# Routing of a mixture-of-experts stage by batch, with tiles given out in order, a GpSimd subtraction and weights read in place

## The chip, the cores and the metric

The kernel runs on one core of one Trainium2 chip. The metric is the device time of that core in microseconds, lower is better. Each number of a profile comes from one profiled execution of the program.

## What is computed

The input `x` has 4 batches of 512 rows of 128 float32 values, and there is a context of 32 rows per batch. Eight layers are added to `x` one after the other, each on the row-normalised `x`:

```python
x = x + L0_xattn(layernorm(x), ctx)      # layer 0: attention, 8 heads, windows
x = x + L0_ffn(layernorm(x))             # layer 1: 8 experts, hidden 512, 1 expert a row
x = x + L1_xattn(layernorm(x), ctx)      # layer 2: attention, 16 heads
x = x + L1_ffn(layernorm(x))             # layer 3: 16 experts, hidden 256, 3 experts a row
x = x + L2_xattn(layernorm(x), ctx)      # layer 4: attention, 16 heads, causal mask
x = x + L2_ffn(layernorm(x))             # layer 5: dense, ternary weights
x = x + L3_xattn(layernorm(x), ctx)      # layer 6: attention, 16 heads, mask
x = x + L3_ffn(layernorm(x))             # layer 7: a table looked up by cluster and tile

# layer 1: top = argmax(logits + gate_b + expert_bias); out = relu(x@w1[e] + b1[e]) @ w2[e] + b2[e] for e = top
# layer 3: g = softmax(x @ gate); keep the 3 largest of 16, divide by their sum;
#          out = sum over the 3 of g[e] * (relu(x@W1[e] + b1[e]) @ W2[e] + b2[e])
```

## The kernel before

**Tiles.** A tile is 128 rows, so there are 16 tiles of `x`, four in each batch. Everything is float32. The program is written by hand for each engine, and the order of the lines is the order of each engine's work. Semaphores are waited on between engines.

**The two expert layers** (1 and 3) work on rows sorted by expert. TensorE computes logits for a batch (`logits`, L1421 to L1430). VectorE then does `gating` (L793 to L853) once for all 16 tiles. It finds the largest logit of each row by `first_largest` (L777 to L790), once for layer 1 and three times for layer 3, and writes one-hot choices. Layer 3 also takes a softmax, for which ScalarE does the exponential (L1285). TensorE's `ranks` (L1576 to L1584) counts by matmul with a triangle of ones how many rows chose each expert so far, in 17 matmuls. VectorE's `route` (L855 to L891) turns that into a slot number for each row and the expert number `es` of each tile of slots. Each expert owns whole tiles. Layer 1 has 24 tiles of slots, layer 3 has 64.

**Scatter and gather.** GpSimd issues indirect DMAs of one tile each. `scatter` (L450 to L457) writes the normalised rows to `xbuf` in DRAM: 16 DMAs for layer 1, 48 for layer 3. It waits on `s_slot`, which `route` raises once for the layer. `gather` (L459 to L465) reads the results back from `ybuf`, as many DMAs. The first gather of a layer waits until all groups of four tiles of the layer are stored. Its destination is the weight buffer `wall`, so the load of layer 3's weights (L410 on SP) waits until layer 1's gathered rows have been added. Between gathers GpSimd does `power` (L440 to L448), the square root of each layer norm: two small operations and one of some 1 us.

**The expert loop** (`moe`) has bodies of 8 tiles. SP loads groups of four tiles from `xbuf` and stores groups to `ybuf` (L386 to L392). TensorE does for tile s: `turn` (a transpose, L1597), then `hidden` for tile s-1 (L1605), then `second` for tile s-2 (L1614). A matmul of 128x128 float32 appears as two instructions in the trace. ScalarE copies the transposed tile (L1253) and does the ReLU (L1260). VectorE reads the eight expert numbers of a body into registers (L953) and for each tile copies the expert's w1 (L926), b1 (L927), w2 (L932) and b2 (L933) out of the whole set of weights with a register in the address, and adds the bias to a finished tile (L917). In layer 1 a tile has 4+4 matmuls and one transpose, in layer 3 it has 2+2 and one transpose.

**Attention** (`period`) is a pipeline over 16 tiles. TensorE makes scores (L1479), VectorE takes the row maximum (L735) and subtracts it (L739), ScalarE does the exponential (L1186), TensorE transposes (L1484), ScalarE copies (L1190), TensorE multiplies (L1495), VectorE normalises (L748, L752) and after four tiles adds to `x` (L556) and takes the statistics of the next norm (L521 to L528). In layer 6 VectorE also applies a mask by a minimum (L733). In layers 2 and 4 the gathered rows of a batch are added (`add_experts`, L893 to L908) in the middle of the attention's pipeline.

**Order around the experts.** Before the loop of layer 1, VectorE does `gating(1)`, `route(1)`, `prepare(2)` (attention weights), `prepare5` and `prepare7` (weights of the layers 5 and 7). Before the loop of layer 3 it does `gating(3)`, `route(3)`, `prepare(4)`, `prepare(6)` and a masked copy (L972). GpSimd's order is:

```python
for l in MOE:
    scatter(l)
    for r in range(2):
        pool.wait_ge(s_ys[r], 16 * (tile_before[l] + SLOT_TILES[l]) // BODY)
    gather(l, 0, 0)
    gather(l, 0, 1)
    for b in range(1, B):
        gather(l, b, 0)
        power(4 * l + 3 + b)
        gather(l, b, 1)
```

## Time and profile before

| | before |
|---|---|
| median of 3 runs | 740.15 us (739.88 to 740.39) |
| the profiled execution, its own time | 738.92 us |
| its span in the trace | 737.1 us |
| TensorE busy | 449.4 us (61%) |
| VectorE busy | 389.1 us (53%) |
| ScalarE busy | 242.0 us (33%) |
| GpSimd busy | 192.3 us (26%) |
| mean granted TensorE clock | 0.768 of full |

Some 1.8 us of the execution's own time lie around the span. "Busy" leaves out register, branch and semaphore instructions. A row of the timeline gives start, duration, engine, line, operation, output and inputs, and in brackets the idle time before it and what ended it. Two neighbouring instructions of VectorE can overlap in the rows by their tails, so what an instruction costs in a row of others is the distance from its start to the next start.

### The profile page before, as it was taken

The numbers are of one execution on the slowest core, as the hardware profiler recorded it, in microseconds if no ns is written. First come the engines' busy times: TensorE is split into PE (matmuls) and PEld (weight loads), VectorE is DVE, ScalarE is ACT, GpSimd is POOL, SyncE is SP. The second block draws the span as 40 slices with busy tenths as digits, with TensorE's granted clock in tenths as the row PEclk, the third lists the DMA queues.
The fourth block names the chain that finished last, engine by engine and source line by source line (L and its number), as shares of the span: only waits on it lengthen the run. The fifth ranks groups of instructions, "written<-read, shape, count | busy, mean of one in ns | idle before, by whom it ended". The sixth has DMA issues, their size and how long they took to land.

```text
span 737.1 us, 9512 instructions
## 1 busy us (share of the span) xinstructions
PE 449.4 (61%) x2662; PEld 353.8 (48%) x2662; DVE 389.1 (53%) x1346; ACT 242.0 (33%) x634; POOL 192.3 (26%) x250
## 2 busy tenths in 40 slices
PE   1935964699268862650068888025578998887070
PEld 1834562499236752410067777013455675774050
DVE  2343538465246836720036666044675659965856
ACT  0011101266144640020046666013334465553023
POOL 3010206200352110277700000586631120013002
PEclk9965557699779975675579999556787999997555
DMA  6493001221110700011123333111100000000001
GB/s 178 103 313 124 0 1 36 64 59 45 49 29 23 270 1 0 11 50 53 53 76 101 99 85 85 50 50 35 36 15 1 1 2 0 1 1 1 0 0 57
DMA packets 55884, 39.86 MB, mean 54 GB/s; under 512 B 8900, under 2 KB 50837, under 8 KB 55718
## 3 DMA queue, kind: packets, MB, share of 16 engines
q1 hardware_dynamic: 51750, 31.01, 14.2%
q0 software_dynamic: 4096, 8.40, 3.9%
q8 instruction: 17, 0.28, 0.2%
q14 instruction: 21, 0.17, 0.1%
HBM read 24.18 MB, written 15.20 MB: 53 GB/s over the span
## 4 chain that ended last, share of the span: by engine, by line
PE 35%; DVE 22%; POOL 15%; issue 10%; DVEq 8%; ACT 6%; DMA 3%; SPq 1%; POOLq 0%; ACTq 0%
POOL xbuf L457 8%; PE bank L1605 6%; PE bank L1614 5%; PE bank L1479 4%; POOL wall L465 3%; DVE e_sb L739 2%; ACT xn L1171 2%; POOL rstd L446 2%; DVE mx L735 2%; DVE stats L521 2%; PE bank L1382 2%; PE bank L1469 2%; PE bank L1582 2%; PE bank L1484 1%; PE bank L1510 1%
## 5 line engine op out<-in xcount | busy, mean ns | idle before, releaser
L465 POOL DMA_INDIRECT wall<-ybuf,slots x64 | 61.5, 961 | 172.1 <-DMA ybuf<-h_sb 96.0
L1260 ACT ACTIVATE r<-bank,b1s 128x128 f32<-128x128 f32 x224 | 67.3, 365 | 49.8 <-PE bank L1605 49.8
L457 POOL DMA_INDIRECT xbuf<-h_sb,slots x64 | 63.4, 991 | 70.8 <-DVE slots L890 51.9
L1605 PE MATMUL bank<-on,e_sb 128*128 128x128 f32 x448 | 70.4, 290 | 13.3 <-DVE b1s L927 12.8
L445 POOL TENSOR_SCALAR nmr<-mv 128x4 f32<-128x4 f32 x32 | 7.8, 244 | 237.8 <-DVE veps L528 236.0
L1605 PEld LDWEIGHTS bank<-on,e_sb 128*128 128x128 f32 x448 | 59.2, 198 | 21.6 <-DVE b1s L927 20.5
L917 DVE TENSOR_TENSOR h_sb<-bank,oT 128x128 f32<-128x128 f32 x88 | 25.5, 289 | 81.8 <-PE bank L1614 81.8
L1614 PE MATMUL bank<-eT,r 128*128 128x128 f32 x448 | 66.1, 280 | 0.6 <-issue 0.6
L1614 PEld LDWEIGHTS bank<-eT,r 128*128 128x128 f32 x448 | 57.8, 194 | 1.7 <-issue 1.1
L1469 PE MATMUL bank<-ident,xn 128*128 128x128 f32 x64 | 13.1, 340 | 74.5 <-ACT xn L1171 74.3
L1597 PE MATMUL bank<-ident,h_sb 128*128 128x128 f32 x88 | 24.7, 286 | 54.3 <-DMA h_sb<-xbuf 54.3
L1171 ACT ACTIVATE xn<-x,nmr,rstd 128x128 f32<-128x128 f32 x64 | 26.3, 481 | 68.6 <-POOL nmr L448 68.6
L1479 PE MATMUL bank<-VW,xnT_all 128*128 128x512 f32 x64 | 45.5, 818 | 5.1 <-ACT xnT_all L1179 3.2
L1495 PE MATMUL bank<-vB,eT 128*128 128x36 f32 x384 | 47.1, 271 | 0.0
L1190 ACT COPY eT<-bank 128x512 f32<-128x512 f32 x48 | 28.1, 584 | 57.7 <-PE bank L1484 57.7
L1495 PEld LDWEIGHTS bank<-vB,eT 128*128 128x128 f32 x384 | 46.9, 194 | 0.0
L1469 PEld LDWEIGHTS bank<-ident,xn 128*128 128x128 f32 x64 | 8.6, 169 | 78.0 <-ACT xn L1171 78.0
L1253 ACT COPY on<-bank 128x128 f32<-128x128 f32 x88 | 23.6, 269 | 65.0 <-PE bank L1597 64.7
L926 DVE COPY e_sb<-wall 128x256 f32 (+1 forms) x88 | 28.9, 328 | 21.9 <-ACT r L1260 11.6
L1597 PEld LDWEIGHTS bank<-ident,h_sb 128*128 128x128 f32 x88 | 12.9, 149 | 56.7 <-DMA h_sb<-xbuf 56.7
L735 DVE TENSOR_REDUCE mx<-bank 128x16 f32<-128x512 f32 x48 | 33.1, 689 | 13.1 <-PE bank L1479 11.0
L1484 PEld LDWEIGHTS bank<-ident,e_sb 128*128 128x128 f32 x192 | 25.7, 152 | 25.0 <-issue 15.0
(262 smaller groups left out, 928.3 us busy)
## 6 DMA issues: line engine op xcount, KB each, us to landing
wall<-in_w SPq DMA_DIRECT2D x4, 2048.0 KB, 12.3
h_sb<-xbuf SPq DMA_DIRECT2D x22, 256.0 KB, 2.8
ybuf<-h_sb SPq DMA_DIRECT2D x22, 256.0 KB, 2.3
xbuf<-zero SPq DMA_DIRECT2D x16, 256.0 KB, 3.7
x<-in_x SPq DMA_DIRECT2D x4, 256.0 KB, 3.7
xbuf<-h_sb,slots POOLq DMA_INDIRECT x64, 2.2
wall<-ybuf,slots POOLq DMA_INDIRECT x64, 2.5
b2all<-in_L_ffn_b SPq DMA_DIRECT2D x1, 1024.0 KB, 15.4
```

Source lines behind the costliest of these rows:

```text
L457: nc.gpsimd.indirect_dma_start(xbuf[0:SLOT_TILES[l] * P], bass.IndirectOffsetOnAxis(slots[:, c:c + 1], 0), tile_of(xn_all, t), None).then_ ...
L465: nc.gpsimd.indirect_dma_start(tile_of(yg, t * K + k), None, ybuf[0:SLOT_TILES[l] * P], bass.IndirectOffsetOnAxis(slots[:, c:c + 1], 0)).t ...
L735: v.tensor_reduce(m, s, AX_X, ALU.max)
L1171: i = a.activation(tile_of(dst, w), tile_of(x, b * W + w), ACT.Identity, bias=nmr[:, w:w + 1], scale=rstd[:, w:w + 1])
L1260: i = a.activation(hT[:, (u % 2) * 512 + c * P:(u % 2) * 512 + (c + 1) * P], bank[2 + u % 2][:, c * P:(c + 1) * P], ACT.Relu, bias=b1s[:, ...
L1469: i = nc.tensor.transpose(tile_of(xT_ps, w), tile_of(src, w), ident[:, :])
L1479: mm(s_ps[t % 2][:, :], tile_of(xnT_all, t), aB[l][:, (t // W) * 512:(t // W + 1) * 512], start=True, stop=True).then_inc(s_s, 1)
L1484: i = nc.tensor.transpose(tile_of(e_ps[t % 2], c), e_sb[:, (t % 2) * 512 + c * P:(t % 2) * 512 + (c + 1) * P], ident[:, :])
L1495: i = mm(o_ps[p % 2][:, at + c * VC:at + (c + 1) * VC], eT[:, (t % 2) * 512 + c * P:(t % 2) * 512 + (c + 1) * P], vB[l][:, ((t // W) * 4 + ...
L1597: nc.tensor.transpose(bank[4 + u % 2][:, 0:P], tile_of(xs, u), ident[:, :]).then_inc(s_xt, 1)
L1605: h = mm(tile_of(bank[2 + u % 2], c), w1s[:, (u % R) * n + c * P:(u % R) * n + (c + 1) * P], tile_of(xsT, u % 2), start=True, stop=True)
L1614: y = mm(bank[6 + u % 2][:, 0:P], hT[:, (u % 2) * 512 + c * P:(u % 2) * 512 + (c + 1) * P], w2s[:, (u % R) * n + c * P:(u % R) * n + (c + ...
```

## The change

- **Routing by batch.** `gating` and `route` take a batch (4 tiles) and run four times a layer, and so do `ranks` (5 matmuls) and, in layer 3, the exponential. `route` gives tiles of slots out in order: an expert that has room left in its last tile fills it first, and a batch adds new tiles behind those of the batches before. It therefore carries `room`, `last_end` and `ends` from batch to batch. In layer 3 the three largest come from the instructions `max` and `max_index`, one each for every tile, where `first_largest` was called three times.
- **Scatter by batch.** GpSimd scatters a batch as soon as its slots are known. In layer 3 the first batch's scatter stands before `power(14)` and `power(15)`, inside attention 2.
- **Gather by batch.** A batch can only have used the first `LIMIT` tiles: 11, 15, 19, 23 of 24 in layer 1, and 27, 39, 51, 63 of 64 in layer 3. Its gather waits for these alone, that is for 3, 4, 5, 6 groups of four tiles in layer 1 and for 7, 10, 13, 16 in layer 3. The gathers of batches 0 to 2 stand before the `power` of the next norm. Destinations are other buffers, and SP's wait for `s_gad` goes.
- **w2 in place.** VectorE no longer copies w2. TensorE loads the expert numbers of a body into its own registers (from `es_late`, shifted by two tiles) and reads w2 out of `wall` with a register in the address of each matmul of `second`.
- **GpSimd subtraction.** In layer 6 VectorE's minimum writes to SBUF (`s_sb`), the maximum reads from there, and GpSimd subtracts.
- **Moved.** `prepare5` and `prepare7` go from before layer 1's loop to before layer 3's loop, behind `prepare(4)` and `prepare(6)`. `prepare(2)` still stands before layer 1's loop.

The diff, cut to its core:

```diff
+LIMIT = {l: [min(SLOT_TILES[l], (512 * TOPK[l] * (b + 1) + MOE[l][0] * (P - 1)) // P) for b in range(B)] for l in MOE}
...
-        yg = wall
+        yg = {1: [vZ[:, b * S:(b + 1) * S] for b in range(B)],
+              3: [h_sb[:, B * S:B * S + 3 * S], vZ[:, 0:3 * S], vZ[:, B * S:B * S + 3 * S], wall[:, 0:3 * S]]}
...
-                    sp.wait_ge(s_gad, 4)
...
+            def scatter(l, b, part):
+                pool.wait_ge(s_slot, (b + 1) if l == 1 else B + b + 1)
+                if l == 1 and b == 0:
+                    pool.wait_ge(s_zero, loads["s_zero"])
+                for w in (2 * part, 2 * part + 1):
+                    for k in range(TOPK[l]):
+                        t = b * W + w
+                        nc.gpsimd.indirect_dma_start(xbuf[0:LIMIT[l][b] * P], bass.IndirectOffsetOnAxis(slots[:, k * T + t:k * T + t + 1], 0), tile_of(xn_all, t), None).then_inc(s_sc_x, 16)
...
             def gather(l, b, part):
                 K = TOPK[l]
+                groups_needed = -(-LIMIT[l][b] // GT)
+                if part == 0:
+                    for r in range(2):
+                        pool.wait_ge(s_ys[r], 16 * (tile_before[l] // BODY + (groups_needed + 1 - r) // 2))
...
+            for n in range(7):
                 power(n)
+            for part in range(2):
+                scatter(1, 0, part)
+            power(7)
+            for b in range(1, B):
+                for part in range(2):
+                    scatter(1, b, part)
+            for b in range(3):
+                gather(1, b, 0)
+                gather(1, b, 1)
+            power(8)
+            power(9)
+            gather(1, 3, 0)
+            gather(1, 3, 1)
+            for n in range(10, 14):
+                power(n)
+            scatter(3, 0, 0)
+            power(14)
+            scatter(3, 0, 1)
+            power(15)
+            for b in range(1, B):
+                for part in range(2):
+                    scatter(3, b, part)
+            for b in range(3):
+                gather(3, b, 0)
+                gather(3, b, 1)
+            power(16)
+            gather(3, 3, 0)
+            power(17)
+            add_bo(0)
+            gather(3, 3, 1)
...
+            def subtract(t):
+                g = att_before[6] * W + t
+                pool.wait_ge(s_mx, t + 1)
+                if t >= 2:
+                    pool.wait_ge(s_e, g - 1)
+                nc.gpsimd.tensor_tensor(tile_of(e_sb, t % 2, 512).rearrange("p (h j) -> p h j", h=H),
+                                        tile_of(s_sb, t % 2, 512).rearrange("p (h j) -> p h j", h=H),
+                                        mx[:, (t % 2) * H:(t % 2 + 1) * H].unsqueeze(2).to_broadcast([P, H, SK]), ALU.subtract).then_inc(s_sub, 1)
...
+            def gating(l, b):
...
+                v.tensor_reduce(most, logit, AX_X, ALU.max)
+                dve.drain()
+                v.tensor_tensor(tiles(gv), logit, most.unsqueeze(2).to_broadcast(w_), ALU.subtract).then_inc(s_gsub, 1)
+                dve.wait_ge(s_gexp, b + 1)
...
+                for w in range(W):
+                    v.max(top[:, w * 8:(w + 1) * 8], gv[:, w * E:(w + 1) * E])
+                dve.drain()
+                for w in range(W):
+                    v.max_index(top_i[:, w * 8:(w + 1) * 8], top[:, w * 8:(w + 1) * 8], gv[:, w * E:(w + 1) * E])
...
+            def route(l, b):
+                dve.wait_ge(s_rank, (b + 1) if l == 1 else B + b + 1)
+                v.tensor_copy(rk[:, 0:n + E], rank_bank(l, b)[:, 0:n + E]).then_inc(s_rk, 1)
...
+                v.tensor_copy(slots[:, :].rearrange("p (k t) -> p k t", k=3)[:, 0:K, b * W:(b + 1) * W],
+                              slot_f[:, 0:K * W].rearrange("p (k w) -> p k w", k=K)).then_inc(s_slot, 1)
+                reached = esc[:, 0:NS * E].rearrange("p (s e) -> p s e", e=E)
+                v.tensor_tensor(reached, number[:, 0:NS].unsqueeze(2).to_broadcast([1, NS, E]), ends[0:1, 0:E].unsqueeze(1).to_broadcast([1, NS, E]), ALU.is_ge)
+                dve.drain()
+                v.tensor_reduce(es_n[:, 0:NS], reached, AX_X, ALU.add)
...
+                if b == B - 1:
...
+                    v.tensor_copy(es_late[:, 2:NS + 2], es_f[:, 0:NS]).then_inc(s_es, 1)
+                    v.tensor_copy(es[:, 0:NS], es_f[:, 0:NS])
...
-            norm(5, 1, tile_of(xn_all, 1, S))
+            stats_of(5, 1)
+            gating(1, 0)
+            normed(5, 1, tile_of(xn_all, 1, S))
             add_y(0, 2)
-            norm(6, 2, tile_of(xn_all, 2, S))
+            stats_of(6, 2)
+            route(1, 0)
+            normed(6, 2, tile_of(xn_all, 2, S))
+            gating(1, 1)
             add_y(0, 3)
-            norm(7, 3, tile_of(xn_all, 3, S))
+            stats_of(7, 3)
+            route(1, 1)
+            normed(7, 3, tile_of(xn_all, 3, S))
+            gating(1, 2)
+            route(1, 2)
+            gating(1, 3)
+            route(1, 3)
...
                 if l == 6:
-                    v.tensor_tensor(s, s, cap6[:, t * SK:(t + 1) * SK].unsqueeze(1).to_broadcast([P, H, SK]), ALU.min)
+                    if t >= 2:
+                        dve.wait_ge(s_sub, g - 1)
+                    kept = tile_of(s_sb, t % 2, 512).rearrange("p (h j) -> p h j", h=H)
+                    v.tensor_tensor(kept, s, cap6[:, t * SK:(t + 1) * SK].unsqueeze(1).to_broadcast([P, H, SK]), ALU.min).then_inc(s_cs, 1)
                     dve.drain()
+                    v.tensor_reduce(m, kept, AX_X, ALU.max).then_inc(s_mx, 1)
+                    return
...
-                        v.tensor_copy(w2s[:, (u % R) * n:(u % R + 1) * n], wall[:, bass.ds(e * n + WHALF, n)])
...
             prepare(2)
+            moe(1)
+            add_experts(1, 1)
+            stats_of(norm_no(2, 1), 1)
+            for t in range(-1, 14):
+                period(2, t)
+            gating(3, 0)
+            period(2, 14)
+            route(3, 0)
+            for t in range(15, 18):
+                period(2, t)
+            gating(3, 1)
+            period(2, 20)
+            route(3, 1)
+            for b in (2, 3):
+                gating(3, b)
+                route(3, b)
+            prepare(4)
+            prepare(6)
+            v.copy_predicated(cap6[:, :], mask_u8[:, :], neg3[:, :])
             for stage in range(4):
                 prepare5(stage)
             prepare7()
...
+            def ranks(l, b):
+                pe.wait_ge(s_sel, (b + 1) if l == 1 else B + b + 1)
...
+                mm(out_[:, 0:(W + 1) * E], tri[:, :], gsel[:, 0:(W + 1) * E], start=True, stop=False, skip_group_check=True)
+                for t in range(W):
+                    i = mm(out_[:, (t + 1) * E:(W + 1) * E].rearrange("p (n e) -> p n e", e=E), ones[:, :],
+                           gsel[:, t * E:(t + 1) * E].unsqueeze(1).to_broadcast([P, W - t, E]), start=False, stop=(t == W - 1), skip_group_check=True)
...
-                pe.wait_ge(s_wd, s + (tb + 1))
...
-                               w2s[:, (u % R) * n + c * P:(u % R) * n + (c + 1) * P], start=(c == 0), stop=(c == C - 1))
+                               wall[:, bass.ds(e * n + (WHALF + c * P), P)], start=(c == 0), stop=(c == C - 1))
...
                 def body(i, peeled):
+                    experts = experts_of(i * BODY, BODY)
...
-                            second(s - 2, (u - 2) % BODY, peeled and u < 4)
+                            second(s - 2, (u - 2) % BODY, peeled and u < 4, experts[u])
```

On TensorE and ScalarE the exponentials, `ranks(3, b)` and `prepare5` are placed to match: `gate_exp(b)` after the periods 13, 17, 21 and 25 of attention 2, `ranks(3, b)` after the periods 14, 18, 21 and 24. On ScalarE the normalising of a batch for layer 3 (L1171, periods 13, 17, 21) stands ahead of `gate_exp`. On TensorE `prepare(2)` stands ahead of layer 1's loop as before.

## Rows read from the trace of the kernel before

**Rows 1.** Busy time by stretch: experts of layer 1, of layer 3, attention 6.

```profile
core 0: us, PE busy (x) PEld busy (x) DVE busy (x) ACT busy (x) POOL busy (x), PEclk, DMA share, GB/s
139.60:190.50 50.90, 48.40 (x408) 47.04 (x408) 28.83 (x119) 31.45 (x120) 0.00 (x0) 0.97 0.17 49
374.00:462.00 88.00, 75.73 (x574) 67.69 (x574) 56.71 (x310) 53.34 (x191) 0.00 (x0) 0.97 0.31 87
607.00:655.00 48.00, 41.80 (x257) 31.21 (x256) 42.87 (x92) 27.27 (x54) 4.46 (x10) 0.96 0.00 1
```

**Rows 2.** Timeline of VectorE: first additions behind each expert loop.

```profile
200.16 0.70 DVE L899 TENSOR_TENSOR x<-x,wall 128x512 f32<-128x512 f32 x1 [9.83 <-DMA wall<-ybuf,slots]
...
481.39 3.57 DVE L906 SCALAR_TENSOR_TENSOR x<-wall,gk,x 128x128 f32<-128x128 f32 x12 [19.49 <-DMA wall<-ybuf,slots]
```

**Rows 3.** Timeline of GpSimd: scatters in layers 1 and 3, an addition.

```profile
134.58 0.96 POOL L457 DMA_INDIRECT xbuf<-h_sb,slots  x1 [0.30 <-issue]
...
323.80 1.02 POOL L457 DMA_INDIRECT xbuf<-h_sb,slots  x1 [0.30 <-issue]
...
496.33 1.27 POOL L470 TENSOR_TENSOR x<-x,bo 128x512 f32<-128x512 f32 x1
```

**Rows 4.** Chain that ended last, layer 3: start us, us, what.

```profile
370.28 2.86 DMA h_sb<-xbuf
```

**Rows 5.** Timeline of TensorE, ScalarE, VectorE ahead of layer 1's loop.

```profile
86.46 1.71 PE L1429 MATMUL bank<-gw,xnT_all 128*128 128x8 f32 x8
...
105.41 5.32 PE L1582 MATMUL bank<-gsel,ones 128*128 128x128 f32 x32
...
123.11 0.58 ACT L1242 COPY VW<-bank 128x512 f32<-128x512 f32 x1 [0.78 <-PE bank L1559]
...
114.49 2.50 DVE L603 TENSOR_TENSOR vZ<-kT,mask 128x512 f32<-128x512 f32 x4 [0.16 <-issue]
```

**Rows 6.** Timeline of VectorE: steps of route in layers 1 and 3.

```profile
111.80 0.22 DVE L871 TENSOR_REDUCE first<-cmp_ 128x8 f32<-128x64 f32 x1
112.09 0.17 DVE L873 TENSOR_TENSOR ends<-first,ntile 128x8 f32<-128x8 f32 x1
112.18 0.17 DVE L874 TENSOR_SCALAR base<-first 128x8 f32<-128x8 f32 x1
...
302.23 1.20 DVE L879 TENSOR_TENSOR A<-number,ends 1x1024 f32<-1x1024 f32 x1
```

**Rows 7.** Timeline: ScalarE's norm in attention 2; VectorE's weight preparation.

```profile
257.11 1.63 ACT L1171 ACTIVATE h_sb<-x,nmr,rstd 128x128 f32<-128x128 f32 x4
...
307.46 0.29 DVE L595 TENSOR_REDUCE wqs<-wq 128x1 f32<-128x128 f32 x1 [0.16 <-issue]
...
322.58 0.28 DVE L926 COPY e_sb<-wall 128x256 f32 x1
...
117.60 0.69 DVE L616 SCALAR_TENSOR_TENSOR ab<-wfc 128x512 f32<-128x512 f32 x1
...
137.94 0.15 DVE L677 TENSOR_SCALAR temp<-temp 128x1 f32<-128x1 f32 x1
```

**Rows 8.** Timeline of TensorE and VectorE in layer 3's loop.

```profile
386.00 0.71 PE L1605 MATMUL bank<-on,e_sb 128*128 128x128 f32 x4 [0.92 <-DVE b1s L927]
...
387.00 0.27 PE L1597 MATMUL bank<-ident,h_sb 128*128 128x128 f32 x1
...
388.00 0.27 PE L1597 MATMUL bank<-ident,h_sb 128*128 128x128 f32 x1
...
396.88 0.71 PE L1605 MATMUL bank<-on,e_sb 128*128 128x128 f32 x4 [1.11 <-DVE b1s L927]
...
385.58 0.29 DVE L926 COPY e_sb<-wall 128x256 f32 x1 [1.09 <-ACT r L1260]
...
388.02 0.29 DVE L926 COPY e_sb<-wall 128x256 f32 x1 [0.20 <-issue]
```

**Rows 9.** Groups of instructions of VectorE in attention 6.

```profile
L739 DVE TENSOR_TENSOR e_sb<-bank,mx 128x512 f32<-128x512 f32 x16 | 11.1, 692 | 1.2
```

More of the change, by code:

```diff
@@ L499, in _ @@
+            for n in range(24, 27):
+                power(n)
+            for t in range(T):
+                subtract(t)
+                if t == 2:
+                    power(27)
+                if t in (9, 13):
+                    power(28 + (t - 9) // W)
+            power(30)
+            power(31)
             pool.wait_ge(s_c7, loads["s_c7"])
@@ L962, in _ @@
             prepare7()
-            moe(1)
-            add_experts(1, 1)
-            stats_of(norm_no(2, 1), 1)
-            for t in range(-1, 21):
-                period(2, t)
-            gating(3)
-            route(3)
-            prepare(4)
-            prepare(6)
-            v.copy_predicated(cap6[:, :], mask_u8[:, :], neg3[:, :])
             moe(3)
@@ L1649, in _ @@
                 prepare(6, stage)
+            for stage in range(3):
+                prepare5(stage)
             moe(3)
```

398 lines of the change are left out of this document (212 added, 186 removed).

## The prediction

> **What bounds the kernel now.** I read the page's slices first, then the chain of waits, then the timeline by engine around each gap. No engine is busy throughout. The time lies in stretches in which one thing is waited for.
>
> Around both expert layers GpSimd's indirect DMAs stand alone. Each takes 0.96 us and 0.30 us between two [rows 3], 1.26 us in all: 16 before layer 1's loop (20 us), 48 before layer 3's (61 us). Layer 3's rows are then loaded at 370.28 and landed at 373.1 [rows 4]. Behind the loops the first additions wait 9.8 us and 19.5 us for gathers [rows 2]. In layer 1's loop TensorE is busy 48.4 of 50.9 us. In layer 3's it is busy 75.7 of 88.0 us and in attention 6 it is 41.8 of 48.0 us, with VectorE at 42.9 [rows 1].
>
> **The change part by part**, against the profiled execution's own 738.92 us. The 1.8 us around the span stay. The median shown is 1.2 us higher.
>
> *A. Ahead of layer 1's loop: +6.4.* A drained step of VectorE on small operands costs 0.29 us, a second operation beside one 0.09 [rows 6]. A batch of layer 1 has a gating of 8 steps, which I take at 0.27 (2.1 us), and a route of some 13 to the slots (4.1) with a tail for the expert numbers (1.4). Ranks are 10 instructions, which at 5.32 us for 32 [rows 5] make 1.7, with the semaphores 2.0. The first logits end at 87.2: four matmuls (8 instructions, 1.71 us) from 85.6, where the output matmul before them ends, near 86.46, where they begin today [rows 5]. Batch 0's slots come at 102.0, since w_out(3), 4.1 us of TensorE, stands before its ranks. After that a batch takes 10 to 11 us: gating, ranks and route in series and the norm between. The slots stand at 113.3, 124.4 and 134.4, and VectorE is through at 136.4. The last four scatters would let the loop begin at 143.4. But `prepare(2)` follows on the same VectorE. It took from 114.49 to 123.7 [rows 5], 9.2 us beside the scatters, and now it has no cover: 145.6. Loading registers on TensorE takes another 0.9 (E), less 0.5 for ScalarE's last copy. The loop begins at 146.0 in place of 139.6. The scatters that get hidden are paid back by that chain.
>
> *B. Layer 1's loop: +1.* TensorE sets it, so VectorE's lost copy buys nothing. Register arithmetic is costed in E.
>
> *C. Behind layer 1: -11.2.* Three batches are gathered in the loop (3, 4 and 5 of 6 groups needed). The 9.8 us go. Another 1.4 go because the addition of batch 1, also late for its gather, made VectorE late for the first scores.
>
> *D. From attention 2 to layer 3's loop: -6.* Gating of batch 0 needs an exponential behind ScalarE's norm that ends at 258.7 [rows 7]. From there: 3.8 for the rest of the gating, 2.0 ranks, 5.0 to the slots, 3.1 for the expert numbers, two of whose steps are 1x1024 at 1.2 each [rows 6]. That is 273.5. Batch 1 waits for the attention's own work (4 us) and for ScalarE, whose next norm needs `power(14)`, and this now stands behind six scatters (8 us) on GpSimd: 299.5. Batches 2 and 3 take gating 4.9, ranks 2.0 and route 8.1 each, and the last 0.7 more: 330.5. The last scatters end at 343.5 with nothing to wait for. But VectorE still owes `prepare(4)` and `(6)`, 15.1 us (307.46 to 322.58), and `prepare5` and `7`, 20.5 us (117.60 to 138.1) [rows 7]. Both were hidden beside scatters and are bare now. VectorE reaches the loop at 366.1, and with its register load at 367, where the rows landed at 373.1. What is late next is VectorE, not the DMAs.
>
> *E. Layer 3's loop: -7.9.* Undisturbed tiles follow at 1.00 us (387.00 to 388.00). Eight of them take 10.88 (386.00 to 396.88), because TensorE waits for weights, 0.92 to 1.11 us at the head of a body [rows 8]. There VectorE spends 1.09 us, of which an ordinary pause is 0.20, so the register load takes 0.89. Without the copy of w2 (0.2) VectorE keeps up with 1.00. TensorE now has the load itself; I take 0.8 of it exposed, so a body costs 8.8. Seven bodies save 14.6 and the first 0.3. Against that stands the arithmetic: three register operations for each address and one more for each tile, 7 a tile in layer 3 and 13 in layer 1, 760 in both. The trace has none in a matmul's address. The bounds are nothing (TensorE's sequencer runs ahead of the array) and the 0.12 us that an address costs VectorE behind a drain (0.20 against 0.08 for a plain step), 0.04 an operation, 30 us for all. I take 0.11 us a tile in layer 3 (7.0 us), because ReLU there ends barely before `second` needs it, and almost nothing in layer 1 (B), where the array is busy longer for each address.
>
> *F. Behind layer 3: -18.6.* Batches 0 to 2 are gathered in the loop (7, 10 and 13 of 16 groups). The 19.5 us of [rows 2] go, and 0.6 of waiting behind gathers. The third batch needs group 13 and 12 DMAs of 1.26, and ends 1.5 us after `power(16)` could start.
>
> *G. Attention 4: 0.* Its later batches found their gathers landed.
>
> *H. Attention 6: -5.* VectorE gives up 16 x 0.61 us, of 0.69 us each [rows 9]. TensorE's 41.8 of 48.0 us is the next bound, so at most 6.2 [rows 1]. GpSimd's 128x512 addition takes 1.27 us [rows 3]. A subtraction at 0.69 to 2.5 us stays under 2.6 us a tile. I take 1.3, and 1 us for the longer first chain.
>
> Sum: 6.4 + 1 - 11.2 - 6 - 7.9 - 18.6 - 5 = -41.3. That is 697.6 against 738.92, and 698.8 as a median.
>
> **A page against a row.** Gathers now run beside VectorE's copies in the loops. The one place where this is seen is a scatter at 323.80: 1.02 against 0.96 us, while copies run on VectorE [rows 3], so I add nothing. The Trainium skill (SBUF — State Buffer, section "SBUF: two separate sides") says that a DMA issued by GpSimd cannot write its descriptors while a float32 copy of VectorE holds the shared port, and gives 3100 ns for one that alone takes 620. An estimate from that page, 2.5 us more for each gather in a loop, would put the sum near 730. This trace does not agree so far, though it has only a few instructions of such overlap.
>
> **The rivals.**
>
> *R1, gathers starve in the loops.* A gather beside copies takes 3.7 us, as if it waited out every copy of a tile. Then some 10 of layer 3's 36 are done when the loop ends, and 26 x 1.26 us follow bare. F falls by 26, C by 6: 731. For it: VectorE copies three times a tile. Against: the row above. 0.10.
>
> *R2, TensorE pays for its addresses.* At the 0.04 us of an operation, all exposed: 760 x 0.04 = 30 in place of 8: 721. For it: the operations stand between wait and matmul. Against: in today's loops TensorE has a wait value to compute for each tile and a branch for each body, and still holds 1.00 us. 0.12.
>
> *R3, slower than before.* The same mechanism at another price. Without any arithmetic the sum is 690.8 as a median. 760 operations, all bare, eat the 49 us from 0.065 us each on. With 0.08 the time is 752. Layer 1 alone would then lose 25 us. Nothing in the rows is that dear. 0.04.
>
> *R4, scatters beside attention in name only.* `max` and `max_index` are in no row. I took 0.12 us between two, 8 a batch. The nearest rows are small operations of 0.15 to 0.29 us, the upper bound 0.69, that of 512 columns [rows 9]. That is up to 4.6 us a batch and 18 in all. Then layer 3's loop starts no earlier than now, or later, and the hiding of 48 scatters brings nothing: 705 to 717, say 713. 0.12.
>
> The forecast has 0.62. Its own range is 682 to 714, which spans the load and arithmetic of E from none to the half of their price, D by 8 either way, and H from 0 to 6.
>
> **The numbers.** The time is that of the forecast, 698.8. The range goes from 681 to 726: it takes in R2 and R4 and leaves out R1, R3 and some of the low end. A measurement of this kernel tells 0.2% from no change, 1.5 us. Faster 0.95, same 0.01, slower 0.04.
>
> **What would show it.** A: layer 1's first transposes near 145 us, with GpSimd idle before them. B and E: layer 1's loop at 1.9 us a tile as now; bodies of layer 3 near 9.7 us, with gaps at the body's head put down to TensorE's own issue. C and F: additions at once behind the last tile. D: VectorE busy without a break from the last `route` to the loop, and TensorE waiting for its copies, not for the load. H: tiles at 2.6 to 2.8 us. The forecast is wrong if layer 1's tile exceeds 2.1 us (R2), if gathers in the loops last over 2 us (R1), or if the loop of layer 3 waits for the load from `xbuf`.

## The result and the profile after

| | before | after |
|---|---|---|
| median, first comparison | 740.27 us | 755.72 us (755.33 to 756.06) |
| ratio | | 1.0208, interval 1.019 to 1.0225 |
| profiled execution, its span | 737.1 us | 754.1 us |
| the changed kernel again, on three more chips | 740.5, 740.7, 741.5 us | 756.8, 697.1, 698.3 us |

The changed kernel was slower by 2.1% where 5.6% less was forecast. That is half of the result. The other half is in the last line: on two of the chips that it met later it took what was forecast, and on a third it was slow again. On one chip its executions agree within 4 us. Between chips the same program differs by up to 60 us, while the kernel before moves by 1 us on these four and by 3.5 us with that of the first set of experiments (743.8 us).

The page of the changed kernel in its first comparison, with the granted clock by slices:

```profile
span 754.1 us, 10056 instructions
PE 472.3 (63%) x2674; PEld 373.3 (50%) x2675; DVE 401.4 (53%) x1532; ACT 242.7 (32%) x637; POOL 211.7 (28%) x268
...
PEclk9955555699788955555779977865677999997555
```

Busy time by stretch, as in [rows 1]: layer 1's loop, layer 3's loop, attention 6.

```profile
144.50:200.00 55.50, 48.99 (x409) 46.70 (x407) 20.09 (x90) 32.06 (x121) 11.40 (x12) 0.98 0.20 58
381.00:506.00 125.00, 87.68 (x574) 77.85 (x574) 49.06 (x257) 53.97 (x190) 34.28 (x36) 0.82 0.28 80
631.00:679.00 48.00, 44.47 (x300) 34.31 (x298) 35.91 (x90) 28.93 (x60) 22.57 (x30) 1.00 0.00 1
```

Layer 3's loop takes 125 us where [rows 1] have 88, with the same 574 matmuls in it. TensorE is busy for 70% of it in place of 86%, VectorE for 39% in place of 64%. The mean granted clock of the stretch is 0.82 in place of 0.97 of full, and TensorE's busy time 87.7 us in place of 75.7. Now VectorE's first additions, that answer to [rows 2], and a gather beside the loop:

```profile
200.28 0.69 DVE L1001 TENSOR_TENSOR x<-x,vZ 128x512 f32<-128x512 f32 x1
...
505.80 3.56 DVE L1008 SCALAR_TENSOR_TENSOR x<-h_sb,gk,x 128x128 f32<-128x128 f32 x12
```

```profile
423.18 0.95 POOL L489 DMA_INDIRECT h_sb<-ybuf,slots  x1 [0.30 <-issue]
424.43 0.94 POOL L489 DMA_INDIRECT h_sb<-ybuf,slots  x1 [0.30 <-issue]
```

The waits of 9.8 and 19.5 us are gone and the gathers go at their old pace of 1.25 us. What happens beside them is in the timeline of the compute engines, around the start of a burst of 12 gathers (421.89 to 436.7) and behind it:

```profile
422.97 0.27 PE L1728 MATMUL bank<-ident,h_sb 128*128 128x128 f32 x1
...
423.32 0.26 ACT L1361 COPY on<-bank 128x128 f32<-128x128 f32 x1
...
424.18 0.27 PE L1728 MATMUL bank<-ident,h_sb 128*128 128x128 f32 x1
...
425.26 0.27 PE L1728 MATMUL bank<-ident,h_sb 128*128 128x128 f32 x1
...
426.16 0.29 DVE L1019 TENSOR_TENSOR h_sb<-bank,oT 128x128 f32<-128x128 f32 x1 [2.04 <-PE bank L1749]
426.19 0.27 ACT L1361 COPY on<-bank 128x128 f32<-128x128 f32 x1 [1.64 <-PE bank L1728]
...
429.02 0.62 ACT L1368 ACTIVATE r<-bank,b1s 128x128 f32<-128x128 f32 x2 [2.56 <-PE bank L1736]
...
430.47 0.42 PE L1728 MATMUL bank<-ident,h_sb 128*128 128x128 f32 x1
...
433.27 0.29 DVE L1019 TENSOR_TENSOR h_sb<-bank,oT 128x128 f32<-128x128 f32 x1 [6.03 <-remote]
...
434.70 0.27 ACT L1361 COPY on<-bank 128x128 f32<-128x128 f32 x1 [5.05 <-remote]
...
439.46 0.27 ACT L1361 COPY on<-bank 128x128 f32<-128x128 f32 x1
```

ScalarE copies (L1361) once for each transpose (L1728), and the trace has 64 of each in the loop, so they can be paired by counting. The transpose of 422.97 ends at 423.24 and is copied at 423.32. That of 424.18 is copied 1.7 us after its end, at 426.19. That of 425.26, over at 425.53, is copied at 434.70, 9.2 us later, and that of 430.47, over at 430.89, at 439.46, 8.6 us later. From the fourth tile on the step takes 0.04 to 0.11 us outside the bursts. (The label "remote" stands where the profile found no end of an instruction close to the signal that ended the wait.) The ends of matmuls are modelled in the profile, so the rows do not tell whether TensorE finishes late or only its signal comes late. I call it a late signal. The additions of VectorE (L1019), which wait for matmuls of TensorE (L1749) in the same way, are up to 8.6 us late in this loop. The transposes follow at 425.26, 430.47 and 440.73, where two tiles take 2.3 us otherwise. The loop has three such bursts. The same shows beside the scatters, in VectorE's own chain of short steps (gating of batch 3, 24 scatters beside it until 331.3):

```profile
320.11 0.22 DVE L801 TENSOR_REDUCE gred<-gv 128x4 f32<-128x64 f32 x1 [0.32 <-issue]
320.99 0.18 DVE L803 RECIPROCAL gred<-gred 128x4 f32<-128x4 f32 x1 [0.66 <-issue]
322.39 0.23 DVE L805 TENSOR_TENSOR gv<-gv,gred 128x64 f32<-128x64 f32 x1 [1.22 <-issue]
...
325.92 0.09 DVE L811 MATCH_VALUE_LOAD top_i<-top,gv 128x8 f32 x1 [2.82 <-issue]
...
332.92 0.18 DVE L815 CAST top_f<-top_i 128x32 f32<-128x32 uint32 x1 [6.18 <-issue]
```

The first 0.32 us are ordinary, a wait for ScalarE's exponential. Of the others, 0.66, 1.22, 2.82 and 6.18 us, each is about twice the one before. They lie in VectorE's drains, the instructions that wait until its own earlier steps are finished. The one ahead of the last row, once in each of the four batches, in ns (smallest, median, largest) and with the start of its first and last:

```profile
L814 DVEq DRAIN  x4: 496/497/6683, 262.0 to 326.2; - x4
```

I call both, the late signals of TensorE and the long drains of VectorE, the pauses.

**Where the time went, step by step.** Distances between marks of the trace in us. The marks are the starts of the loops' first transposes (for layer 3, where TensorE then still waits for VectorE, the first `hidden`), the last bias additions, the first row maximum of attention 2, the first addition behind layer 3, the first minimum of attention 6 and the end.

| stretch (term) | before | after | change | the same kernel on a chip without pauses | change | forecast |
|---|---|---|---|---|---|---|
| start to layer 1's loop (A) | 139.66 | 144.54 | +4.9 | 145.31 | +5.7 | +6.4 |
| loop 1 (B) | 50.38 | 55.36 | +5.0 | 49.51 | -0.9 | +1 |
| to the first maximum (C) | 20.46 | 10.62 | -9.8 | 10.62 | -9.8 | -11.2 |
| to layer 3's first `hidden` (D) | 163.56 | 171.12 | +7.6 | 160.69 | -2.9 | -6 |
| loop 3 (E) | 87.55 | 123.78 | +36.2 | 82.79 | -4.8 | -7.9 |
| to the first addition (F) | 19.78 | 0.38 | -19.4 | 0.38 | -19.4 | -18.6 |
| attention 4, layer 5 (G) | 126.79 | 126.44 | -0.4 | 123.69 | -3.1 | 0 |
| attention 6 and layer 7 (H) | 128.92 | 121.86 | -7.1 | 122.21 | -6.7 | -5 |
| sum | 737.1 | 754.1 | +17.0 | 695.2 | -41.9 | -41.3 |

The two kernels of the last columns are one program. They differ in B, D and E by 57 us, which is where bursts of indirect DMAs stand beside chains of short work.

### The profile page after: what moved, and what is told of

Same layout as the page of the kernel before. It is cut to its first block, busy times and chain, and to the rows that moved or that the text cites. A ratio compares the mean times of both kernels' runs of the same rounds, so it can differ in the third digit from the quotient of the medians.

```text
span 754.1 us, 10056 instructions
## 1 busy us (share of the span) xinstructions
PE 472.3 (63%) x2674; PEld 373.3 (50%) x2675; DVE 401.4 (53%) x1532; ACT 242.7 (32%) x637; POOL 211.7 (28%) x268
## 4 chain that ended last, share of the span: by engine, by line
PE 45%; DVE 22%; issue 11%; ACT 7%; DVEq 6%; POOL 5%; another core or an unknown queue 4%; SPq 1%; DMA 0%; ACTq 0%; POOLq 0%
PE bank L1736 8%; PE bank L1749 8%; PE bank L1620 6%; ACT xn L1279 3%; PE bank L1636 2%; POOL rstd L465 2%; PE bank L1625 2%; PE bank L1502 2%; PE bank L1728 2%; DVE stats L581 2%; PE bank L1608 2%; PE bank L1563 2%; DVE x L1008 1%; PE bank L1887 1%
## 5 line engine op out<-in xcount | busy, mean ns | idle before, releaser
L1736 PE MATMUL bank<-on,e_sb 128*128 128x128 f32 x448 | 74.2, 301 | 22.3 <-DVE b1s L1029 13.6
L477 POOL DMA_INDIRECT xbuf<-h_sb,slots x64 | 65.8, 1029 | 70.3 <-DVE slots L883 53.0
L1749 PE MATMUL bank<-wall,r 128*128 x448 | 72.6, 297 | 20.1 <-ACT r L1368 13.1
L1736 PEld LDWEIGHTS bank<-on,e_sb 128*128 128x128 f32 x448 | 62.2, 206 | 30.1 <-DVE b1s L1029 16.6
L1749 PEld LDWEIGHTS bank<-wall,r 128*128 128x128 f32 x448 | 62.1, 206 | 22.7 <-issue 22.6
L1019 DVE TENSOR_TENSOR h_sb<-bank,oT 128x128 f32<-128x128 f32 x88 | 25.6, 291 | 88.2 <-PE bank L1749 54.0
L489 POOL DMA_INDIRECT vZ<-ybuf,slots x40 | 38.1, 953 | 82.0 <-DMA ybuf<-h_sb 71.1
L1361 ACT COPY on<-bank 128x128 f32<-128x128 f32 x88 | 23.5, 269 | 43.5 <-PE bank L1728 32.8
L1561 PE MATMUL bank<-gsel,tri 128*128 128x40 f32 (+1 forms) x16 | 5.5, 443 | 50.2 <-DVE gsel L827 42.2
L1294 ACT ACTIVATE e_sb<-e_sb 128x512 f32<-128x512 f32 x48 | 30.3, 632 | 15.6 <-DVE e_sb L957 9.1
L581 DVE BATCH_NORM_STATS2 stats<-x 128x6 f32<-128x128 f32 x128 | 27.9, 280 | 13.7 <-DMA x<-in_x 10.9
L1625 PE MATMUL bank<-ident,e_sb 128*128 128x128 f32 x192 | 32.7, 298 | 2.5 <-ACT e_sb L1294 2.4
## 6 DMA issues: line engine op xcount, KB each, us to landing
wall<-in_w SPq DMA_DIRECT2D x4, 2048.0 KB, 12.5
```

Of the source, the lines that this page charges most:

```text
L477: nc.gpsimd.indirect_dma_start(xbuf[0:LIMIT[l][b] * P], bass.IndirectOffsetOnAxis(slots[:, k * T + t:k * T + t + 1], 0), tile_of(xn_all, t ...
L489: nc.gpsimd.indirect_dma_start(tile_of(yg[l][b], w * K + k), None, ybuf[0:LIMIT[l][b] * P], bass.IndirectOffsetOnAxis(slots[:, c:c + 1], 0 ...
L581: v.bn_stats(stats[:, w * 6:w * 6 + 6], src(w))
L1294: a.activation(e, e, ACT.Exp, scale=1.0 if l == 2 else DH ** -0.5).then_inc(s_exp, 1)
L1625: i = nc.tensor.transpose(tile_of(e_ps[t % 2], c), e_sb[:, (t % 2) * 512 + c * P:(t % 2) * 512 + (c + 1) * P], ident[:, :])
L1736: h = mm(tile_of(bank[2 + u % 2], c), w1s[:, (u % R) * n + c * P:(u % R) * n + (c + 1) * P], tile_of(xsT, u % 2), start=True, stop=True)
```

## The experiments

Five sets, each on a chip of its own, each with the kernel before beside it. The first four kernels are the changed kernel with one edit.

**e1_gather_late.**

```diff
-            for b in range(3):
-                gather(3, b, 0)
-                gather(3, b, 1)
-            power(16)
...
+            for r in range(2):
+                pool.wait_ge(s_ys[r], 16 * (tile_before[3] + SLOT_TILES[3]) // BODY)
+            gather(3, 0, 0)
+            gather(3, 0, 1)
+            for b in range(1, B):
+                gather(3, b, 0)
+                power(15 + b)
+                gather(3, b, 1)
+                add_bo(b - 1)
```

> The changed kernel, with layer 3's gathers and powers in the order of the kernel before and all behind the last stored group, so that no gather runs beside layer 3's loop. Theory T (a burst of GpSimd's gathers holds up the other engines, which wait for each other tile by tile): the loop, 129.7 us from its first transpose to its last addition, falls to 64 tiles of 1.26 us and its ends, some 86 us; the wait for the first gathers comes back with about 19.5 us; the time is near 732 us. Rival U (the matmuls with a register in their address and TensorE's register loads make the loop slow): the loop stays near 130 us and the time rises to some 775 us.

**e2_gather_paced.**

```diff
...
+            stored(0)
+            for j in range(12):
+                pool.wait_ge(s_my, tile_before[3] + 30 + 2 * j)
+                one_gather(0, j)
+            stored(1)
+            for j in range(4):
+                pool.wait_ge(s_my, tile_before[3] + 54 + 2 * j)
+                one_gather(1, j)
             power(16)
...
```

> The changed kernel, with batch 0's gathers and four of batch 1's beside layer 3's loop one for every two tiles (each waits for TensorE's tile count), the rest behind it between the powers. Theory T in its form for bursts (only gathers that follow each other closely hold the engines up): the loop takes some 86 to 90 us, the wait for the first gathers stays away, the time is near 713 us. Rival V (every gather beside the loop costs it some 1.2 us, close together or not, 36 of them 43 us): 16 gathers cost 19 us, the loop takes 105 us, the time is near 732 us. Rival U: the loop stays near 130 us.

**e3_w2_copied** (the edit of the change taken back, on VectorE and TensorE).

```diff
+                        v.tensor_copy(w2s[:, (u % R) * n:(u % R + 1) * n], wall[:, bass.ds(e * n + WHALF, n)])
...
-                               wall[:, bass.ds(e * n + (WHALF + c * P), P)], start=(c == 0), stop=(c == C - 1))
+                               w2s[:, (u % R) * n + c * P:(u % R) * n + (c + 1) * P], start=(c == 0), stop=(c == C - 1))
```

> The changed kernel, with VectorE's copy of w2 put back and the registers and addresses taken off TensorE, gathers beside the loop as in the changed kernel. Theory T: layer 3's loop still stands in its three bursts of gathers and takes 125 to 135 us, the time is 752 to 762 us. Rival U: the loop falls to some 88 us, as in the kernel before, and the time to 714 us.

**e4_scatter_late.**

```diff
-            scatter(3, 0, 0)
             power(14)
-            scatter(3, 0, 1)
             power(15)
-            for b in range(1, B):
+            pool.wait_ge(s_slot, 2 * B)
+            for b in range(B):
```

> The changed kernel, with layer 3's 48 scatters all behind the last batch's slots, so that none runs beside attention 2 and the routing. Theory T: the pauses of VectorE between 319 and 333 us, some 12 us in all in a chain of short steps, go, and so do a few us of waiting for ScalarE around 280 and 292 us; the last slots come some 14 us earlier than 342.5 us, near 328 us; 48 scatters of 1.265 us then stand bare, the loop starts near 393 us in place of 375.7, and the time is near 773 us. Rival W (those pauses have another cause than the scatters): the last slots still come at 342 us, the loop starts near 407 us, and the time is near 787 us.

Measured, the kernel before at 743.8 us beside them:

| | time | ratio (interval) | layer 3's loop |
|---|---|---|---|
| e1 | 739.1 us | 0.9931 (0.9903 to 0.996) | 81.7 us |
| e2 | 722.5 us | 0.9721 (0.968 to 0.9763) | 84.3 us |
| e3 | 765.0 us | 1.0288 (1.0239 to 1.0336) | 129.9 us |
| e4 | 774.9 us | 1.042 (1.037 to 1.047) | 125.6 us |

Busy time by stretch of layer 3's loop, e1, e2 and e3 in turn:

```profile
383.50:465.30 81.80, 76.97 (x574) 69.42 (x574) 47.45 (x254) 54.07 (x190) 0.00 (x0) 0.97 0.33 93
```

```profile
386.70:471.20 84.50, 78.72 (x574) 69.77 (x574) 48.40 (x255) 53.94 (x190) 15.12 (x16) 0.97 0.39 103
```

```profile
383.40:513.50 130.10, 85.80 (x574) 76.65 (x574) 59.19 (x319) 53.16 (x190) 34.09 (x36) 0.81 0.27 77
```

What differs with the loop's length is GpSimd's column: no gather, 16 gathers 2.4 to 3.4 us apart, 36 gathers 1.25 us apart. With 16 spaced gathers the loop is 2.6 us longer than with none, where one price per gather (V) gives 19. U is out: without any register work on TensorE the loop still stands. e4 says the same of the scatters. Its gating of batch 3 is undisturbed, and the last slots come at 328.91 where the changed kernel has 342.46. But the 48 scatters now stand beside VectorE's preparation of weights (329.4 to 391.4), and the pauses moved there. One and the same step of it in e4 and, from the fourth set, in the changed kernel on a chip without pauses:

```profile
369.71 0.69 DVE L697 COPY wfcT<-bank 128x512 f32<-128x512 f32 x1 [16.05 <-remote]
```

```profile
351.57 0.69 DVE L698 COPY wfcT<-bank 128x512 f32<-128x512 f32 x1 [1.27 <-PE bank L1709]
```

From the last slots to layer 3's first `hidden` VectorE takes 70 us in e4 and 39 to 40 us there and in the changed kernel of the first comparison. (The wait of 7.1 us that the expectation of f1 takes for such a pause is not one: it stands in the kernel before and in h1 as well, 7.04 and 7.07 us.) The time was forecast within 2 us. In e1 the 19.4 us wait is back, as expected. Its time is 7 us over the expected, 3.5 of which the kernel before shows too in this set.

**The second set** started from e2.

**f1_hold_scatter.**

```diff
+            scatter(3, 1, 0)
+            scatter(3, 1, 1)
+            pool.wait_ge(s_slot, 2 * B)
+            for b in (2, 3):
```

> The kernel with paced gathers (e2_gather_paced, 722.5 us), with the scatters of layer 3's batches 2 and 3 held until the last slots are known. Theory T (VectorE's pauses of 3.1 and 6.2 us in the gating of batch 3 belong to the burst of 24 scatters beside it): the pauses go, the last slots come some 14 us earlier, 24 scatters of 1.265 us then end near 360 us, before VectorE is ready, and the loop starts some 12 us earlier: 710 us. Rival X (the pauses only move: VectorE's weight preparation stands beside the held burst instead, as one step did for 7.1 us in e4_scatter_late): the loop starts 5 us earlier, 717 us, or not at all earlier, 722 us.

**f2_sub_vector.** Layer 6's `max_sub` and GpSimd's order as in the kernel before.

```diff
-                    v.tensor_tensor(kept, s, cap6[:, t * SK:(t + 1) * SK].unsqueeze(1).to_broadcast([P, H, SK]), ALU.min).then_inc(s_cs, 1)
+                    v.tensor_tensor(s, s, cap6[:, t * SK:(t + 1) * SK].unsqueeze(1).to_broadcast([P, H, SK]), ALU.min)
```

> The kernel with paced gathers (722.5 us), with layer 6's subtraction back on VectorE and its minimum back in the bank. From the stretch between the first minimum of attention 6 and the end, 129.8 us in the kernel before and 122.7 us in the changed kernel, the subtraction on GpSimd is worth 7 us: 729.5 us. Rival (the prediction's term H): 5 us, 727.5 us. Rival (the gain comes from elsewhere in that stretch): 722.5 us.

**f3_prepare7_late.**

```diff
-            prepare7()
             moe(3)
...
             for t in range(-1, 18):
                 period(4, t)
+                if t == 2:
+                    prepare7()
```

> The kernel with paced gathers (722.5 us), with prepare7 (4.6 us of short steps of VectorE) moved from ahead of layer 3's loop into attention 4, where VectorE waits 7.4 us for TensorE in each batch. If VectorE's bare preparation sets the start of the loop, as term D of the prediction has it, 4.4 us go: 718 us. Rival (the scattered rows or the weights set it): the time stays at 722.5 us.

**f4_gather_fours.**

```diff
...
+                if j % 4 == 0:
+                    pool.wait_ge(s_my, tile_before[3] + 30 + 2 * j)
...
```

> The kernel with paced gathers (722.5 us), with the same 16 gathers beside the same tiles, but four close together in every eight tiles. Theory T with a start of the pauses some 3.5 us into a burst, as the trace of the changed kernel shows it: each four of 5 us costs the loop 1 to 1.5 us, the loop grows from 84.3 to some 90 us, the time to 728 us. Rival Y (only the mean rate of the gathers counts): 722.5 us. Rival Z (each gather beyond the first in a burst costs its whole 1.25 us): 12 x 1.25 = 15 us, 737 us.

Measured, with 741.2 us for the kernel before: f1 700.3 us (ratio 0.9455), f2 706.7 (0.9526), f3 697.1 (0.9403), f4 696.9 (0.9395), with intervals of 0.003 to 0.004 to each side. All four lie 16 to 26 us under e2, f4 too, which was expected above it. The traces say why: in none of them is there a pause. Layer 1's loop takes 48.3 us from first `hidden` to the last `second`, where e2 has 52.7, and the last slots come at 326 us also in f2 to f4, which keep the scatters beside the routing. The base was missing in the set, so the expected differences from 722.5 us can't be judged. What can be compared is inside the set. From attention 6's first minimum to the end f2 takes 128.1 us and the others 122.1 to 122.3: the subtraction on GpSimd is worth 6 us. f3 reaches layer 3's first `hidden` at 359.8 us, f4 at 366.2 and f2 at 366.6. So VectorE's bare preparation does set the loop's start (some 4 us less of it, 6.4 us earlier in this pair), but f3's time is no better than f4's, whose loop is 2.8 us shorter.

**The third set** brought the changed kernel and e2 again, unchanged, with two combinations.

> The changed kernel itself once more, because the second set of runs came from another chip than the first and showed no pause at all, neither in the routing beside the scatters nor in layer 1's loop beside the gathers. Theory T-chip (the pauses beside bursts of indirect DMAs belong to some chips, not to the kernel): on a chip without them layer 3's loop takes some 84 us with its three bursts of gathers, the last slots come some 13 us earlier, and the time is near 698 us; on a chip with them it is 755 us as before. Theory T-kernel (bursts always hold the loop up and the set of runs only avoided them): 755 us less the routing's pauses, 740 us, with the loop at 124 us.

> The kernel with paced gathers once more, 722.5 us in the first set. T-chip: on a chip without pauses 700 us, the same as the changed kernel beside it within 3 us; on one with them 722 us. T-kernel: 700 us, 40 us under the changed kernel beside it.

> Gathers in fours beside layer 3's loop, and prepare7 in attention 4. If the gains of the second set add up (fours 696.9 us; prepare7 4.4 us): 692.5 us on a chip without pauses, some 715 us on one with them. Rival (prepare7 in attention 4 delays its first batches as much as it frees the loop's start): 697 us.

> Gathers in fours, with w2 copied by VectorE again and no register work on TensorE, on a loop that no burst disturbs. If w2 in place is worth the prediction's term E (7.9 us in layer 3, -1 in layer 1): 7 us more than with w2 in place, 704 us on a chip without pauses. If TensorE's register work eats the gain: 697 us. If layer 1 gains too (its loop took 48.4 us in place of 49.4 us): 705 us.

| kernel before 740.5 us | time | ratio (interval) | layer 3's loop |
|---|---|---|---|
| g1 | 756.8 us | 1.0213 (1.0183 to 1.0242) | 124.1 us |
| g2 | 719.2 us | 0.9721 (0.969 to 0.9752) | 84.0 us |
| g3 | 725.7 us | 0.9792 (0.975 to 0.9834) | 96.6 us |
| g4 | 725.2 us | 0.9787 (0.9729 to 0.9845) | 94.1 us |

This chip has the pauses. Here fours cost what the second set could not show. The loop of g3 is 12.5 us longer than that of g2, 3 us for each burst of four. Its timeline of TensorE and GpSimd at the first of them:

```profile
418.84 0.95 POOL L525 DMA_INDIRECT h_sb<-ybuf,slots  x1 [0.31 <-issue]
420.09 0.98 POOL L525 DMA_INDIRECT h_sb<-ybuf,slots  x1 [0.30 <-issue]
...
421.12 0.71 PE L1759 MATMUL bank<-on,e_sb 128*128 128x128 f32 x4 [1.07 <-issue]
422.84 0.71 PE L1772 MATMUL bank<-wall,r 128*128 x4 [1.01 <-ACT r L1391]
```

g4 against g3 differs in two edits and in the lengths of its pauses, and tells nothing of w2.

**The fourth and fifth set.** h1 and i3 are the changed kernel. h2 and i2 hold all that the runs pointed to (e2, f1, f3, and layer 1's gathers one for each tile). h3 and i1 are the kernel before with this:

```diff
...
+                if l == 1:
+                    pool.wait_ge(s_my, 4)
+                    for j in range(12):
+                        nc.gpsimd.indirect_dma_start(tile_of(extra, j), None, xbuf[0:SLOT_TILES[1] * P], bass.IndirectOffsetOnAxis(slots[:, j:j + 1], 0)).then_inc(s_extra, 16)
```

> The changed kernel a third time, as the measure for the two runs beside it. If this chip has the pauses: 755 to 757 us, layer 3's loop at 124 us. If it has none: 698 us, the loop at some 84 us.

> All that the runs so far point to at once: layer 3's gathers one for every two tiles; layer 1's gathers of batches 0 and 1 one for every tile and batch 2's behind the loop; layer 3's scatters of batches 2 and 3 held until the last slots are known; prepare7 in attention 4. On a chip with pauses, from the 719.2 us of the paced kernel: layer 1's loop 4 us shorter, the routing of batch 3 without its pauses 10 us (13 less one pause that moves to the weight preparation), prepare7 4.4 us: 701 us. On a chip without pauses: 696 us. Rival (held scatters bring a new, longer pause to the preparation of the weights): 710 us.

> The kernel before with 12 gathers added on GpSimd beside layer 1's loop, from its fifth tile on, whose rows go to a buffer of their own that nobody reads; nothing waits for them. Theory T (a burst of indirect DMAs alone holds the loop up, whatever else the change does): on a chip with pauses layer 1's loop, 50.4 us, grows by 8 to 14 us and the time to some 751 us. Rival T-after (the pauses need something of the changed kernel, such as TensorE's register loads, or results written and read at the same time): the loop stays at 50.4 us and the time at 740.5 us. On a chip without pauses both give 740.5 us.

> The kernel before with 12 gathers that nobody needs beside layer 1's loop, again, for a chip with pauses (on one without, the loop took 50.2 us, as without them). Theory T (a burst alone does it): the loop grows from 50 us to 58 to 64 us and the kernel by as much. Rival T-after (the changed kernel's own work is needed): 50 us. If this chip has no pauses either, both give 50 us and the question stays open.

> Everything paced or held, for a chip with pauses (697.9 us on one without). Theory T: without any long burst beside short steps the chip hardly matters: 701 us, layer 1's loop at 49 us, layer 3's at 85 us, last slots near 327 us. Rival (held scatters give the pauses to the preparation of the weights): up to 710 us.

> The changed kernel as the measure: 755 to 757 us if this chip has the pauses (layer 3's loop at 124 us), 697 us if not (83 us).

| | time | ratio (interval) |
|---|---|---|
| h1, changed kernel | 697.1 us | 0.9432 (0.9402 to 0.9462) |
| h2, all paced | 697.9 us | 0.9424 (0.9394 to 0.9454) |
| h3, before with 12 gathers | 745.1 us | 1.0054 (1.0025 to 1.0084) |
| i3, changed kernel | 698.3 us | 0.9413 (0.9372 to 0.9454) |
| i2, all paced | 698.3 us | 0.9414 (0.9373 to 0.9455) |
| i1, before with 12 gathers | 744.1 us | 1.0038 (1.0008 to 1.0068) |

Neither chip has the pauses. In h1 the bursts are at least as long as in the first comparison (12 and 24 gathers in place of three times 12, 36 scatters without a break in place of 24 and 12), and the loop and VectorE's chain run through them:

```profile
366.00:449.00 83.00, 77.65 (x574) 69.54 (x574) 49.62 (x255) 53.93 (x190) 31.10 (x33) 0.97 0.43 117
```

```profile
407.86 0.95 POOL L489 DMA_INDIRECT h_sb<-ybuf,slots  x1 [0.30 <-issue]
409.12 0.94 POOL L489 DMA_INDIRECT h_sb<-ybuf,slots  x1 [0.30 <-issue]
```

```profile
315.30 0.41 DVE L808 MAX8 top<-gv 128x8 f32<-128x16 f32 x4
315.78 0.09 DVE L811 MATCH_VALUE_LOAD top_i<-top,gv 128x8 f32 x1
...
316.59 0.18 DVE L815 CAST top_f<-top_i 128x32 f32<-128x32 uint32 x1
```

The steps before and after `max_index`, 2.8 and 6.2 us late in the first comparison, follow at once. Pacing everything neither gains nor costs here (h2 against h1, i2 against i3): layer 3's loop starts 1 to 3 us earlier and takes 2 us more. No version was clearly faster than the changed kernel on a chip without pauses. On one with them e2 is 37.6 us faster than the changed kernel (g2 against g1) and 2.8% faster than the kernel before. h2 itself met no chip with pauses. The 12 idle gathers in the kernel before left layer 1's loop at 51.2 and 51.4 us for 50.4, and the whole 0.4 to 0.5% longer, on chips where no burst disturbs anything. So whether a burst alone, without anything else of the changed kernel, makes the pauses stays open.

## Why the prediction was wrong

The wrong step stands under "A page against a row": "Gathers now run beside VectorE's copies in the loops. The one place where this is seen is a scatter at 323.80: 1.02 against 0.96 us, while copies run on VectorE [rows 3], so I add nothing." That row answers whether the DMA suffers. Whether the others suffer was not asked, so B, D and E have no term for it. The row itself was a fair witness of the DMA: gathers and scatters keep their 1.25 us, with few exceptions, on every chip, in the pauses too. The cost lies with the engines beside them, as TensorE's signals and VectorE's drains that come late. Between the two columns above it is 41 us in layer 3's loop, 6 in layer 1's and 10 in the routing. It was there in the first comparison and on the chips of the first and third set, and not on the other three. e1 and e2 take the burst away from layer 3's loop, on a chip with pauses, and the loop takes 82 and 84 us. Side by side on one chip it takes 124.1 us with the bursts (g1) and 84.0 with 16 gathers paced and the rest behind it (g2). The trace of before could hardly show it, and whether its chip had the pauses is not on record. Its VectorE is through with the preparation 15 us into the 48 scatters (307.6 to 322.6), where e4's first late signal comes 18 us into the same burst, and behind that the loop waits for the scatters alone. In attention 4, beside bursts of 6 to 14 gathers, the pauses cost little: its second, third and fourth batch begin 21.9, 20.5 and 22.7 us behind the one before in e2, and 21.3, 20.6 and 22.8 us in h2, which has the same gathers on a chip without pauses.

The Trainium skill (SBUF — State Buffer, section "SBUF: two separate sides") has the shared port the other way round, with the GpSimd DMA as the one that waits for VectorE's copies. By that rule the gathers would stretch. The rows disagree: 0.94 to 1.07 us in the loops on both kinds of chips. And what is late are signals of TensorE, an engine that by the same section of the Trainium skill never waits for a port. So that lock is not what these rows show.

Term by term, by the column of the chip without pauses:

- **A and C** held within 1.4 us. Layer 1's first scatters of the batches, at 102.78, 113.69, 125.29 and 135.12 in the first comparison, follow the forecast slots (102.0, 113.3, 124.4, 134.4) within 0.9 us.
- **D** was half right. VectorE, not the rows, set the start of the loop, but came some 4 us later than worked out (h1, counted from attention 2's first maximum): 3 with batch 1's route, 1 with batches 2 and 3. Its preparation took the 35 us of the forecast.
- **E** was mis-sized by 2 to 3 us. A tile takes 1.13 us for the 1.00 and 0.11 of the forecast, the register load 0.83 (1.96 less 1.13) for 0.8, but the first tile of a body takes 1.30. A body has 10.05 us for 9.7, seven times, and the bursts may cost another us: -5.9 in e1 without gathers, -4.8 in h1, on two chips. The body in h1:

```profile
396.29 0.32 PE L1728 MATMUL bank<-ident,h_sb 128*128 128x128 f32 x1 [0.64 <-issue]
...
397.59 0.27 PE L1728 MATMUL bank<-ident,h_sb 128*128 128x128 f32 x1
...
404.38 0.27 PE L1728 MATMUL bank<-ident,h_sb 128*128 128x128 f32 x1
...
406.34 0.32 PE L1728 MATMUL bank<-ident,h_sb 128*128 128x128 f32 x1 [0.63 <-issue]
```

- **F** -19.4 for -18.6, on every chip. **H** -6 to -7 for -5. GpSimd's subtraction takes 1.05 us, and the tiles' minima follow each other at 2.4 us on average (1.4 to 3.7) where they took 2.9, below the 2.6 to 2.8 of the forecast. The group of the first comparison:

```profile
L545 POOL TENSOR_TENSOR e_sb<-s_sb,mx 128x512 f32<-128x512 f32 x16 | 16.8, 1048 | 15.1 <-DVE mx L951 15.1
```

- **G** 0 on one such chip (126.7 us in i3) and -3.1 on the other.

Of the rivals, R1 had the right place and the wrong victim. It said that gathers starve beside copies. What is held up is the work beside them, on some chips. R2 and R3 (register arithmetic) fell with e3, where the loop takes 130 us without the arithmetic, and with h1, where the arithmetic costs layer 3 0.13 us a tile and layer 1 nothing that shows. R3's time, 752, came out near the result by another mechanism, which is luck. R4 fell on the rows of h1: four `max` take 0.41 us and four `max_index` 0.7 (315.78 to 316.46).

The chance of 0.04 for slower was too small, and the reason could have been read: the change moves 48 gathers into loops in which the trace of before has none.

## What to carry to other kernels

When an operation is moved beside others, ask the trace in both directions: does it slow down, and do they. If the trace has no such overlap of the same kind (many short steps that wait for each other beside a long burst), the price is open and the range has to hold it. Spacing the burst by a wait on the neighbour's own count costs 2 us here, and on the chips with pauses it took them out of the loop (e2, g2). Moving a burst can move its cost along with it (e4). And a comparison needs its base on the same chip, in the same set.

## What the hardware showed that was not expected

On the chips of the first comparison and of the first and third set, a burst of GpSimd's indirect DMAs 1.25 us apart makes signals of TensorE come late and drains of VectorE long, and every engine that waits for them stands, SP too. From the end of a transpose to its copy on ScalarE at most 0.13 us pass in both loops (from the fourth tile on) in every trace of the second, fourth and fifth set. On the chips with pauses it is up to 3.2 us beside bursts of four gathers (layer 1's loop, 2.9 to 3.2 in each of the nine traces), and beside bursts of twelve up to 9.2 and 9.8 us in the changed kernel, 12.7 in e3 and 13.6 in e4. VectorE's drains take up to 7.6 us longer (e1, g2). Beside the loops the first late transposes are those that end 2 to 4 us into a burst. Beside the routing 13 us or more pass first. As a rule the pauses end 1 to 3 us behind the burst. With gathers 2.4 to 3.4 us apart (e2, g2) nothing of it is seen in the loop. On the chips of the second, fourth and fifth set the same programs show none. What differs between the chips is not in the records and stays open, as does what holds the signals and the drains back. Every execution here was also recorded by the profiler, so whether the recording has a part in it can't be told either.
